# Flamingo block on one core: 128 eight-byte scatters that each wait for the one before in their list, and three turnings and an eviction of the convolution moved in program order

## The reference

```python
kv  = einsum('bhil,bhjl->bijhl', k_, v_)              # 64 heads of 8 rows, length 1024; k = v = ctx
out = irfft(rfft(kv, 2L) * rfft(ssm_kernel, 2L))[:L] + kv * D
out = einsum('bijhl,bhil->bjhl', out, q_)             # q = layernorm(x)
x   = x + tanh(g_xattn[0]) * out

z      = layernorm(x)                                 # T = 8192 tokens of 1024
aff    = sigmoid(z @ gate_w + expert_bias)            # 7 routed experts, top 2 of each token,
                                                      # then the first T / 7 tokens of each expert by score
shared = (z @ w1a) * silu(z @ w1b) @ w2               # all tokens
routed = the same with each expert's own weights, on its chosen tokens, times their weight
x      = x + tanh(g_ffn[0]) * (shared + scatter_add(routed))
```

## Time and profile before

| | before |
|---|---|
| median of 3 executions | 4221.76 us (4221.09 to 4223.56) |
| the profiled execution: its own time | 4218.65 us |
| its span in the profile | 4217.0 us |
| busy share of the span: PE, DVE, ACT, POOL | 95%, 64%, 45%, 34% |
| mean granted clock of PE | 0.979 |
| matmuls | 24346 |
| chain that ended last | PE 47%, issue 5%, DVE 2%, ACT 1% |

### The profile page before, as it was taken

The page is one execution under the profiler, slowest core; times in us unless marked ns, Lnnn a source line. Parts: engine busy times, 40 slices in busy tenths (PEclk is TensorE's granted clock), DMA queues, the critical chain, the costliest instruction groups (busy, mean ns, idle before and its releaser), DMA issues.

```text
span 4217.0 us, 68165 instructions
## 1 busy us (share of the span) xinstructions
PE 4023.1 (95%) x24346; PEld 3683.4 (87%) x24346; DVE 2717.6 (64%) x3103; ACT 1878.8 (45%) x2441; POOL 1427.6 (34%) x1275
## 2 busy tenths in 40 slices
PE   8999999999999999989999996199999999999999
PEld 7999999999999999967777875178899998999997
DVE  8999999999999999954545563023334343344342
ACT  7888888888888888731111110011112122122120
POOL 2444444544444444401010004710123333333331
PEclk9999999999999999999999998599999999999999
DMA  7888888888888888855552322142364444445443
GB/s 189 215 213 207 212 215 213 212 208 212 215 212 208 210 213 213 208 150 169 176 176 79 120 74 61 30 99 90 94 158 105 92 106 108 85 107 112 92 92 46
DMA packets 292116, 631.99 MB, mean 150 GB/s; under 512 B 33290, under 2 KB 132074, under 8 KB 291976
## 3 DMA queue, kind: packets, MB, share of 16 engines
q0 software_dynamic: 70096, 250.00, 30.8%
q1 hardware_dynamic: 221880, 380.03, 29.8%
HBM read 344.77 MB, written 136.37 MB: 114 GB/s over the span
## 4 chain that ended last, share of the span: by engine, by line
PE 47%; issue 5%; DVE 2%; ACT 1%; another core or an unknown queue 1%; DMA 0%; SPq 0%; POOL 0%; DVEq 0%; PEldq 0%; POOLq 0%
PE mem_acc L2077 11%; PE mem_acc L2078 10%; PE mem_acc L2079 10%; PE moe_ps L2117 3%; PE moe_ps L2119 3%; PE moe_ps L2118 3%; PE moe_psT L2117 2%; PE moe_psT L2118 2%; PE moe_psT L2119 2%; PE moe_psT L2092 1%; ACT moe_zh L1644 1%; DVE moe_y L1989 0%; DVE moe_zin L1950 0%; DVE moe_zl L1902 0%
## 5 line engine op out<-in xcount | busy, mean ns | idle before, releaser
L2077 PE MATMUL mem_acc<-moe_zh,moe_w1h 128*128 128x512 f32 (+2 forms) x2336 | 850.2, 364 | 16.6 <-issue 8.1
L2078 PE MATMUL mem_acc<-moe_zl,moe_w1h 128*128 128x512 f32 (+2 forms) x2336 | 843.7, 361 | 0.8 <-issue 0.8
L2079 PE MATMUL mem_acc<-moe_zh,moe_w1l 128*128 128x512 f32 (+2 forms) x2336 | 842.7, 361 | 1.5 <-issue 1.5
L871 PE MATMUL mem_acc<-att_kv_hi,att_tz_hi 128*128 128x288 f32 x2560 | 768.5, 300 | 20.4 <-DVE mem_pick L810 17.9
L873 PE MATMUL mem_acc<-att_kv_hi,att_tz_lo 128*128 128x288 f32 x2560 | 756.6, 296 | 0.0
L872 PE MATMUL mem_acc<-att_kv_lo,att_tz_hi 128*128 128x288 f32 x2560 | 755.7, 295 | 0.0
L1975 DVE TENSOR_TENSOR moe_hid<-mem_acc,moe_act_s 128x512 f32<-128x512 f32 (+2 forms) x148 | 91.5, 618 | 768.9 <-PE mem_acc L2079 408.8
L871 PEld LDWEIGHTS mem_acc<-att_kv_hi,att_tz_hi 128*128 128x128 f32 x2560 | 481.9, 188 | 41.0 <-DVE mem_pick L810 17.9
L2077 PEld LDWEIGHTS mem_acc<-moe_zh,moe_w1h 128*128 128x128 f32 x2336 | 440.9, 189 | 71.2 <-issue 32.3
L1658 ACT ACTIVATE moe_act_s<-mem_acc 128x512 f32<-128x512 f32 (+2 forms) x148 | 80.0, 540 | 924.1 <-PE mem_acc L2079 889.2
L872 PEld LDWEIGHTS mem_acc<-att_kv_lo,att_tz_hi 128*128 128x128 f32 x2560 | 482.1, 188 | 0.0
(11 more groups left out here) (242 smaller groups left out, 8592.3 us busy)
## 6 DMA issues: line engine op xcount, KB each, us to landing
att_kv_lo<-att_kv POOLq DMA_DIRECT2D x126, 1152.0 KB, 10.3
att_kT<-in_cT SPq DMA_DIRECT2D x64, 512.0 KB, 8.1
att_xn<-in_x SPq DMA_DIRECT2D x64, 512.0 KB, 5.8
out<-att_x SPq DMA_DIRECT2D x64, 512.0 KB, 5.0
z_d<-att_z SPq DMA_DIRECT2D x256, 128.0 KB
moe_y<-out SPq DMA_DIRECT2D x128, 256.0 KB
moe_raw<-z_d POOLq DMA_DIRECT2D x64, 512.0 KB, 4.5
out<-moe_y SPq DMA_DIRECT2D x128, 256.0 KB
```

The source lines that it names most:

```text
L871: nc.tensor.matmul(acc, w_hi[:, cols], x_hi, start=start, stop=False, skip_group_check=True)
L2077: nc.tensor.matmul(acc, w1h[j][:, c, b, :], zh[:, c, 0:w], start=(c == 0), stop=False)
L2078: nc.tensor.matmul(acc, w1h[j][:, c, b, :], zl[:, c, 0:w], start=False, stop=False)
L2079: last = nc.tensor.matmul(acc, w1l[j][:, c, b, :], zh[:, c, 0:w], start=False, stop=(c == C - 1))
```

## The change

Five things are rewritten; no instruction is added or removed but one kind of wait.

1. POOL: ahead of the scatter of column h into list n stands a wait for `scattered[n] >= 16 * h`, that is until all earlier scatters into the same list have landed.
2. PE, each head: `turn_o(h - 1, 0)` stands behind `conv` 0 and no longer behind `conv` 1; `turn_x(h, 1)` stands behind `shared(h, u, 1)` and no longer in the middle of `conv` 5.
3. ACT, each head: `conv_out(h, 0)` is first, ahead of `normal_x1(h - 2)` and `squares(h + 1, 0)`; `queries(h, u, 1)` comes behind the two copies `minus_v(h, 1, ...)`.
4. The last head, ACT and DVE: the first two `ffn_z_high` come behind `queries(h, u, 0)`, the third one later; DVE does `residual(h - 1, 1)` ahead of the first `ffn_z_low`.
5. The last head, SP: the first loads for the experts' stage come ahead of `store_z(h - 2)`.

Outside the lines shown, line numbers of the changed kernel are one higher from L389 to the scatters.

The pieces below are, in this order, from SP, ACT (two), DVE, PE and POOL.

```diff
@@ -383,15 +383,16 @@
             def step(h, u, ahead, back, back2):
+                if not ahead:
+                    sp.wait_ge(z_out, 64 * (h - 2))
+                    load_ffn_z(0)
+                    load_ffn_z(1)
+                    load_ffn_w1(0)
                 if back2:
                     store_z(h - 2)
                 if not (isinstance(h, int) and h >= H - 2):
                     load_keys(h + 2)
                 if not ahead:
-                    sp.wait_ge(z_out, 64 * (h - 2))
-                    load_ffn_z(0)
-                    load_ffn_z(1)
-                    load_ffn_w1(0)
                     load_ffn_z(2)
                     load_ffn_z(3)
@@ -605,11 +606,11 @@
             def step(h, u, ahead, back, back2):
+                conv_out(h, 0)
                 if back2:
                     normal_x1(h - 2)
                 if ahead:
                     squares(h + 1, 0)
-                conv_out(h, 0)
                 conv_out(h, 1)
@@ -622,24 +623,23 @@
                 if ahead:
                     squares(h + 1, 1)
-                else:
-                    ffn_z_high(0)
-                    ffn_z_high(1)
                 conv_out(h, 4)
                 queries(h, u, 0)
                 if not ahead:
-                    ffn_w1_high(0, 1)
-                queries(h, u, 1)
+                    ffn_z_high(0)
+                    ffn_z_high(1)
                 if ahead:
                     high(h + 1, 1 - u, 1)
                 else:
-                    ffn_z_high(2)
+                    ffn_w1_high(0, 1)
                 conv_out(h, 5)
                 minus_v(h, 1, 0)
                 minus_v(h, 1, 1)
+                queries(h, u, 1)
                 if ahead:
                     minus_high(h + 1, 1 - u, 1)
                 else:
+                    ffn_z_high(2)
                     ffn_z_high(3)
                     ffn_w1_high(0, 0)
@@ -828,17 +828,17 @@
                     ffn_z_turn(0)
                     ffn_z_turn(1)
+                if back:
+                    residual(h - 1, 1 - u, 1)
+                if not ahead:
                     ffn_z_low(0)
                     ffn_z_low(1)
                     ffn_w1_low(0, 1)
-                if back:
-                    residual(h - 1, 1 - u, 1)
-                if not ahead:
                     ffn_z_turn(2)
                     ffn_z_turn(3)
-                    ffn_z_low(2)
                 multiply(h, u, 0)
                 if not ahead:
+                    ffn_z_low(2)
                     ffn_z_low(3)
                     ffn_w1_low(0, 0)
@@ -947,14 +947,13 @@
                 def turnings():
-                    turn_x(h, 1)
                     if back:
                         turn_o(h - 1, 1)
 
                 conv(h, u, 0)
-                conv(h, u, 1)
                 if back:
                     turn_o(h - 1, 0)
+                conv(h, u, 1)
                 conv(h, u, 2)
                 conv(h, u, 3)
                 shared(h, u, 0)
                 conv(h, u, 4)
                 turn_x(h, 0)
                 conv(h, u, 5, turnings)
                 shared(h, u, 1)
+                turn_x(h, 1)
                 conv(h, u, 6)
@@ -1519,6 +1519,7 @@
             for h in range(H):
                 for n in range(2):
+                    wait(pool, scattered[n], 16 * h)
                     nc.gpsimd.indirect_dma_start(list_of[n], bass.IndirectOffsetOnAxis(slot_of[:, h, n:n + 1], 0),
                                                  pay[:, h, n, :], None).then_inc(scattered[n], 16)
```

## The result

| | before | after |
|---|---|---|
| median of three executions | 4221.76 us | 4114.04 us (4109.99 to 4115.82) |
| ratio, 95% interval | | 0.9742 (0.972 to 0.9764) |
| span of the profiled execution | 4217.0 us | 4112.4 us |
| busy share of the span: PE, DVE | 95%, 64% | 97%, 66% |
| mean granted clock of PE | 0.979 | 0.988 |

The account below looks back on a forecast made before the run. PE was taken to bound the kernel, with a 148.15 us hole made by POOL's scatters. 4218.65 - 148.15 + 8 - 19 - 4 = 4055.5, plus 3.1 to the median, gave 4059 us; range 4035 to 4225.

Parts of the forecast that it names:

- the likeliest case: Whole kernel: pacing closes PE's hole during the scatters; 4059 us, own range 4035 to 4085, chance 0.42.
- the second rival: Scatter phase: the hole closes in part, PE gets half of it back; 4125 us, 4085 to 4185, chance 0.15.
- The rival by the rule of the Trainium skill: Scatter phase: DMA engines alternate between queues, so thinning the scatters gives nothing; 4199 us, the third rival's time, chance 0.21.
- a fifth fewer (3.1 us a pair for 2.52) closes the hole: POOL's scatters: the landing wait slows each pair to 3.1 us, enough to close the 148.15 us hole.
- 8 us left: Scatter phase: what first and last scatters and 14 list loads may still cost after closure, half of 16 us.
- The closing by rate itself: Scatter phase: something fills in 20 us when arrivals outpace its drain; a slower rate closes the 148 us hole.
- The fourth rival: Scatter phase: the hole stays and grows with the longer phase; 4233 us at 3.1 us a pair, chance 0.19.
- 19 us were forecast: Convolution: moved turnings and earlier first eviction save 0.30 us for each of 62 heads; bounds 0 and 37.
- The cap by DVE: Convolution: DVE has 7.41 us idle in ten heads, of which only the 3.3 us at L742 go away.
- no PEld wait on L542: Convolution, sign of being right: the weight loads' 2.4 us wait for sign copies in ten heads disappears.
- 5.20 + 1.29 us: Last head: PE's two stops, of which reordered evictions, queries and loads were to save 4 us; bounds 0 and 7.
- the third's: Third rival: pacing does nothing, only convolution and last head gain; 4199 us, chance 0.21; 0.02 of it counted as "same".

Follow-up runs that it names:

- the sweep: Changed kernel without the waits for landings, with 4, 2, 1, then 0 memsets behind a scatter; chip 0: 4087.89 us, ratio 0.9685 to the kernel before.
- experiment 2: Changed kernel without the waits between scatters; chip 9: 4053.19 us, ratio 0.9948 to the kernel before.

## Why the prediction was right, and where it was not

The range held, and the forecast of the likeliest case did not: it came out as the second rival (closed in part, 4085 to 4185, chance 0.15).

*What bounds the kernel.* Right for these chips: the scatters make the hole, and it is one of pace. The rival by the rule of the Trainium skill ("DMA: Bandwidth & Descriptors", Queues, rings and completion order) fell for the hole: thinning the scatters closes it. The rule itself is not touched. That the DMA engines have work for 14% of the time and, by that rule, take turns does not save PE, since nothing shows that PE was short of transfers. The loads that the first four results in the hole need besides PE's products were issued from 2546.54 to 2553.6, some 49 us before the first of these results (2602.89). Their landing is not in the trace, so that DVE's "remote" is late news of a product, as I had it, is likely and not shown. In the changed kernel's hole it hardly occurs (3.0 us on DVE, 9.8 us on ACT), while the matmuls let go one by one are there again. These are the more direct sign.

*The step that failed* is "a fifth fewer (3.1 us a pair for 2.52) closes the hole". The mean was sized well: 127 steps in 207.4 us are 3.27 us a pair. But I spread it evenly. The wait is 0 whenever the landing is in time, and it was in time for 63 us on end, at 2.6 us a pair. My bound had said so ("between 2.52 us (the wait costs nothing)"), and the sum then used the middle. Where waits do occur they were longer than the 0.58 us I added (43.8 / 25 = 1.75 us in the mean, up to 3.4), in the stretches in which other transfers run. So the term "8 us left" measured 62.

*The closing by rate itself* was argued from one number, the 20 us until the hole opens. It is now shown by the spaced scatters (hole gone at 1.8 us), and the sweep agrees.

*The fourth rival* (hole grows with the phase) did not come: where scatters were slow, PE ran undisturbed.

*Convolution.* 19 us were forecast and 19.08 measured in the profiled executions; by medians 21. The cap by DVE was right in size: it is now busy for 270.80 of 275.80 us, 98.2%. The working was half wrong. The early eviction alone gives 13.7 us, and most of DVE's wait goes with it. Of the 3.3 us read as DVE's wait for the turned result, 1.2 us had "issue" as releaser, and they are still there. And the moved turnings do not cover PE's wait for the sign copies: it went from 2.4 us to 3.1 on the weight loads and 1.2 on PE, so the sign "no PEld wait on L542" failed.

*Last head.* 4 us forecast, none measured. The step that failed is the one that set the 5.20 + 1.29 us against DVE's chain: PE's wait moved from `turn_x` to `ffn_product` and to the first group, whose operands did not come sooner.

*The chances.* The fourth rival's 0.06 and the third's 0.02 make 0.08 for "same", and 0.13 is left for "slower"; the text has 0.07 and 0.14.

*What stays open.* Why chips differ, and what is filled. The landing times that are missing on chips 3 and 0 and present on chip 9 may mean that there events are carried away more slowly. The Trainium skill ("NOTIFIC — the notification-queue block", section 3. Interfaces) says that the block that writes out the engines' records can hold back the producers when a buffer in it fills, and so stall an engine; that would fit matmuls let go one by one with no semaphore to wait for, late news to DVE, and a count by DMAs. No run here shows it: no execution was timed without its records. So it is open, too, whether the hole is there when nothing is recorded. A late supply of instructions is another possibility that no run tests. In the 160 us of the hole the profile's instruction queues (q8, q14) move one packet, and in the same window of experiment 2 nine, but engines that stand still also need fewer.

## What to carry to other kernels

A wait for the transfer before the last bounds what is in flight and not the pace; if the landing comes as soon as the next issue anyway, the wait does nothing, and here that was just where the stream is densest. When a burst stops an engine only after it has run for a while, spread it evenly (here with work of no use on the issuing engine, 1.8 us a DMA), as long as its consumers have slack. Run the kernel before beside every variant, on the same chip: an effect of 148 us was there on two chips and not on a third.

## What was not expected of the hardware

- Indirect DMAs issued by GpSimd every 1.26 us stop PE after 20 us on two chips (148 us in this kernel) and not on a third (PE busy 140.00 of 140.00 us with the same stream).
- At 1.8 us a DMA they never do, in 232 us. At 1.50 us PE ran on for 42 us, but then 6 us at 1.26 were enough; whether the 42 us or the transfers beside the last 6 did that is open.
- 48 DMAs are enough, of 64 rows or of 128, writes or reads of 8 bytes a row: holes of 57.9 and 54.4 us. But 120 DMAs of SP with 128 rows of 8 bytes, one each 1.5 us in the mean, left PE busy for 176.00 of 176.00 us.
- While held, PE starts most matmuls 1.4 to 2.8 us apart, with no releaser in the profile. SP's stores lie up to 32 us apart, since they wait for DVE's results.
